# Second attention of a two-layer decoder: the gate chain over four engines, and the weighed sums formed in quarters

## The reference, cut to what matters

```
q, k, v = x@q_w + q_b, x@k_w + k_b, x@v_w + v_b      # 16 heads of 8
gate    = 1/(1+exp(-(g0 + ...)))                      # per query and head, from q and grep_w
score   = q.k*scale + gate*rel_bias                   # 128 x 128 per head, and one column for bias_k
p       = softmax(score);  attn = p @ v               # 128 queries x 8 per head
out     = layernorm(x + attn@out_w + out_b)           # no gain or offset
```

## Time and profile before

| | |
|---|---|
| median of 3 runs | 5442.01 us (5440.87 to 5447.32) |
| the profiled execution | 5440.75 us, span 5438.9 us |
| second attention in the span | from about 2452 to about 3430 us |
| PE / DVE / ACT / POOL busy over the whole span | 77% / 66% / 41% / 35% |
| the pow of the gate chain (L1380), POOL | 2929 ns, once per sequence |
| Exp of a head's scores (L1572), ACT | 393 ns, 16 per sequence |

### The profile page before, as it was taken

How to read it: one execution, slowest core, us unless ns; L and a number is a source line. 1 busy time by engine, 2 the same in 40 slices (tenths; PEclk the granted TensorE clock), 3 DMA queues, 4 the chain that set the end, 5 groups by cost and what they waited for, 6 DMA issues and landing times. The chain is left out here.

```text
span 5438.9 us, 100417 instructions
## 1 busy us (share of the span) xinstructions
PE 4180.3 (77%) x31987; PEld 2761.0 (51%) x31987; DVE 3586.4 (66%) x9085; ACT 2216.1 (41%) x4986; POOL 1928.3 (35%) x2355
## 2 busy tenths in 40 slices
PE   7888888878885666637888889677773299999998
PEld 3555555555554444435666666566663144444443
DVE  6556565645554555537888887455556688888888
ACT  1444444431111222205666666222221255555555
POOL 1000000024540000007777777000000077777777
PEclk9999999985555555556766776666665599999999
DMA  2000000000100000010000000011111366666564
GB/s 61 9 8 8 10 8 8 8 18 28 29 21 26 23 23 23 23 40 17 13 14 14 13 14 9 28 31 31 29 30 37 93 152 136 134 132 133 134 138 99
DMA packets 261738, 245.27 MB, mean 45 GB/s; under 512 B 28491, under 2 KB 188016, under 8 KB 261490
## 3 DMA queue, kind: packets, MB, share of 16 engines
q1 hardware_dynamic: 252402, 239.73, 18.3%
q10 hardware_dynamic: 9216, 4.20, 0.3%
HBM read 210.27 MB, written 33.55 MB: 45 GB/s over the span
## 5 line engine op out<-in xcount | busy, mean ns | idle before, releaser
L2324 POOL TENSOR_TENSOR d_hidden<-d_gated,d_upper 128x512 f32<-128x512 f32 x528 | 803.7, 1547 | 244.8 <-DVE d_upper L2433 103.1
L2440 DVE TENSOR_TENSOR d_h_low<-d_hidden,d_h_high 128x512 f16<-128x512 f32 x528 | 540.2, 1023 | 135.2 <-ACT d_h_high L2400 133.6
L2394 ACT ACTIVATE d_gated<-d_g 128x512 f32<-128x512 f32 x528 | 315.2, 597 | 479.8 <-PE d_u L2340 455.3
L2433 DVE TENSOR_TENSOR d_upper<-d_u,d_coef 128x512 f32<-128x512 f32 x512 | 349.0, 682 | 31.4 <-DMA d_coef<-coefT 11.8
L706 POOL MEMSET f_minus_half<- 128x1 f32 x1 | 0.1, 98 | 1027.5 <-POOLq L37 1027.5
L1572 ACT ACTIVATE c_sc<-c_sc,c_negmax 128x129 f32<-128x129 f32 x1024 | 326.3, 393 | 15.1 <-issue 11.9
L2400 ACT ACTIVATE d_h_high<-d_hidden 128x512 f16<-128x512 f32 x528 | 328.4, 622 | 8.2 <-POOL d_hidden L2324 8.2
L129 POOL TENSOR_TENSOR b_rstd<-b_var_eps,b_minus_half 128x1 f32<-128x1 f32 x128 | 67.1, 549 | 664.4 <-DVE b_var_eps L119 664.4
L129 POOL TENSOR_TENSOR d_rstd<-d_var_eps,d_minus_half 128x1 f32<-128x1 f32 x64 | 34.1, 548 | 677.4 <-DVE d_var_eps L119 677.4
L1392 POOL TENSOR_TENSOR c_posg<-w_pos,c_gate 128x512 f32<-128x512 f32 x256 | 265.7, 1039 | 3.1 <-issue 3.1
L2338 PE MATMUL d_g<-d_x_high,w_Wg_high 128*128 128x512 f16 x528 | 201.1, 381 | 83.7 <-POOL d_x_low L2317 38.7
(11 more groups left out here) (408 smaller groups left out, 11610.4 us busy)
## 6 DMA issues: line engine op xcount, KB each, us to landing
d_coef<-coefT SPq DMA_DIRECT2D x256, 512.0 KB, 7.6
mx_x<-in_xT SPq DMA_DIRECT2D x16, 256.0 KB, 2.8
b_x<-in_x SPq DMA_DIRECT2D x64, 64.0 KB, 1.8
y<-b_y SPq DMA_DIRECT2D x64, 64.0 KB, 1.6
f_y<-y SPq DMA_DIRECT2D x64, 64.0 KB, 1.9
f_x<-in_x SPq DMA_DIRECT2D x64, 64.0 KB, 1.9
x<-f_res SPq DMA_DIRECT2D x64, 64.0 KB, 1.5
b_x<-x SPq DMA_DIRECT2D x64, 64.0 KB, 1.8
```

The source lines that it names most:

```text
L2324: nc.gpsimd.tensor_tensor(hidden[b][:], gated[b][:], upper[b][:], ALU.mult).then_inc(h_ready, 1)
L2394: nc.scalar.activation(gated[b][:], ps_g[i][:], ACT.Silu, scale=1.0 / W_SCALE).then_inc(silu_ready, 1)
L2433: nc.vector.tensor_tensor(upper[b][:], ps_u[i][:], coef[c % CBUFS][:, u % CU, :], ALU.mult).then_inc(upper_ready, 1)
L2440: nc.vector.tensor_tensor(h_low[b][:], hidden[b][:], h_high[b][:], ALU.subtract).then_inc(h_low_ready, 1)
```

## The change

It has three parts, all in `phase_attn1`.

1. The gate chain. The Exp stays on ACT; the addition of 1 moves from POOL to ACT (an Identity with bias 1.0); the reciprocal moves from a pow with -1 on POOL to a reciprocal on DVE (`invert_gates`, in quarter 1 after `bias`). The small multiplication that fills `gate_rhs` moves from DVE, after its big transpose, to POOL (`gate_columns`, first in quarter 0 of the next column), and PE's `gates_and_values` waits for it.
2. `weigh` is split in four. Quarter `a` of the heads is weighed in quarter `a` of the column, the last part at the place where all 16 stood.
3. `combine`, `turn_attn` and `output` write the free half of the bank `ahead` (columns 256 to 511) instead of `back`. For that PE gets waits on `kv_next_ready`, `x_added` and `attn_ready`, and parts change places. PE: `project` goes from the front of quarter 1 to its end, `turn_attn` from quarter 1 to 2, `output` from 2 to 3. ACT: `copy_attn` from quarter 1 to the end of quarter 2, `norm` from 0 to 1, `store` from 1 to 2. DVE: `add_x` from quarter 2 to after `turn_rows` in 3. POOL: `power` from the end of 3 to quarter 0 of the next column.

The unused branches around `SHIFTED` (an empty tuple before) go too. The diff, cut to its core:

```diff
 # POOL
+    def gate_columns(it, j):
+        pool.wait_ge(rows_ready, nth(it, j))
+        nc.gpsimd.tensor_tensor(gate_rhs[s][:, :, 4:8], rows[s][:, NEXT, 0:4]..., w["quarter"]..., ALU.mult).then_inc(rhs_ready, 1)
     def gates(it, j):
-        nc.gpsimd.tensor_scalar(gate[s][:], gate[s][:], 1.0, None, ALU.add).then_inc(gate_added, 1)
-        nc.gpsimd.tensor_tensor(gate[s][:], gate[s][:], minus_ones[:], ALU.pow).then_inc(gate_inverted, 1)
         pool.wait_ge(gate_inverted, nth(it, j))
 # PE
     def project(it, j):
+        if not is_early(it, j, 4):
+            pe.wait_ge(attn_ready, nth(it, j) - 4)
     def gates_and_values(it, j):
-        pe.wait_ge(rows_ready, nth(it, j))
+        pe.wait_ge(rhs_ready, nth(it, j))
-    def weigh(it, j):
+    def weigh(it, j, a):
+        if a == 0:
+            pe.wait_ge(v_ready, nth(it, j))
+            if not is_early(it, j, 1):
+                pe.wait_ge(weighed_copied, nth(it, j) - 1)
+        pe.wait_ge(pT_copied, quarter(it, j, a))
+        for i in range(4):
+            last = nc.tensor.matmul(back[32 * i:32 * i + 32, a * T:(a + 1) * T], ...)
     def combine(it, j):
+        pe.wait_ge(x_added, nth(it, j) - 1)
+        pe.wait_ge(kv_next_ready, nth(it, j) + 3)
-        out = back[:, 128:128 + H * (HD + 1)]
+        out = ahead[:, 256:256 + H * (HD + 1)]
     def turn_attn(it, j):
+        pe.wait_ge(kv_next_ready, nth(it, j) + 4)
-        nc.tensor.transpose(back[:, 0:T], ...)
+        nc.tensor.transpose(ahead[:, 256:384], ...)
     def step(...):
         if a == 0:
             run(gates_and_values, ahead1)
+            run(weigh, behind1, 0)
             run(combine, behind2)
         if a == 1:
-            run(project, ahead2)
             run(scores, column, 2)
             run(turn, behind1, 3)
-            run(turn_attn, behind2)
+            run(weigh, behind1, 1)
+            run(project, ahead2)
         if a == 2:
             run(scores, column, 3)
             run(turn, column, 0)
-            run(output, behind2)
+            run(weigh, behind1, 2)
+            run(turn_attn, behind2)
         if a == 3:
             run(scores, ahead1, 0)
             run(turn, column, 1)
+            run(output, behind2)
             run(turn_last, behind1)
-            run(weigh, behind1)
+            run(weigh, behind1, 3)
 # ACT
+    act.wait_ge(gate_exp, nth(it, j))
+    nc.scalar.activation(gate[s][:], gate[s][:], ACT.Identity, bias=1.0).then_inc(gate_added, 1)
 # DVE
+    def invert_gates(it, j):
+        dve.wait_ge(gate_added, nth(it, j))
+        nc.vector.reciprocal(gate[s][:], gate[s][:]).then_inc(gate_inverted, 1)
```

More of the change, by code:

```diff
@@ L1323, in pv @@
         def pv(out):
-            return back[:, 128:128 + H * (HD + 1)].rearrange("p (h e) -> p h e", h=H)[out]
+            return ahead[:, 256:256 + H * (HD + 1)].rearrange("p (h e) -> p h e", h=H)[out]
         EVERY = slice(0, P)
@@ L1412, in step @@
                 def step(a, ahead2, ahead1, column, behind1, behind2, behind3):
+                    if a == 0:
+                        run(gate_columns, ahead1)
                     if a == 2:
@@ L1512, in turn_attn @@
                     pe.wait_ge(attn_ready, nth(it, j))
-                    nc.tensor.transpose(back[:, 0:T], attn[slot(j)][:].rearrange("p h e -> p (h e)"), w["ident"][:]).then_inc(attnT_ready, 1)
+                    if not (isinstance(it, int) and U * it + j >= S - 4):
+                        pe.wait_ge(kv_next_ready, nth(it, j) + 4)
+                    nc.tensor.transpose(ahead[:, 256:384], attn[slot(j)][:].rearrange("p h e -> p (h e)"), w["ident"][:]).then_inc(attnT_ready, 1)
                 def output(it, j):
                     pe.wait_ge(attnT_copied, nth(it, j))
-                    nc.tensor.matmul(back[:, 128:128 + D], attnT[slot(j)][:], w["out_w"][:], start=True, stop=True).then_inc(out_ready, 1)
+                    nc.tensor.matmul(ahead[:, 384:512], attnT[slot(j)][:], w["out_w"][:], start=True, stop=True).then_inc(out_ready, 1)
                 def step(a, ahead2, ahead1, column, behind1, behind2, behind3):
@@ L1592, in copy_attn @@
                     act.wait_ge(attnT_ready, nth(it, j))
-                    nc.scalar.activation(attnT[slot(j)][:], back[:, 0:T], ACT.Copy).then_inc(attnT_copied, 1)
+                    nc.scalar.activation(attnT[slot(j)][:], ahead[:, 256:384], ACT.Copy).then_inc(attnT_copied, 1)
                 def norm(it, j):
@@ L1617, in step @@
                         run(copy_turned, behind1, 3)
-                        run(copy_attn, behind2)
-                        run(store, behind3)
+                        run(norm, behind3)
                     if a == 2:
@@ L1623, in step @@
                         run(copy_turned, column, 0)
+                        run(store, behind3)
+                        run(copy_attn, behind2)
                     if a == 3:
@@ L1659, in turn_rows @@
                 def turn_rows(it, j):
[L1660 removed]
+                    s = slot(j)
                     dve.wait_ge(low_ready, nth(it, j))
[L1662 to L1665 removed]
+                    nc.vector.transpose(rows[s][:].rearrange("p b t -> p (b t)"), padded[s][:].rearrange("p b t -> p (b t)")).then_inc(rows_ready, 1)
+                def invert_gates(it, j):
+                    s = slot(j)
+                    dve.wait_ge(gate_added, nth(it, j))
+                    nc.vector.reciprocal(gate[s][:], gate[s][:]).then_inc(gate_inverted, 1)
                 def last_score(it, j):
@@ L1714, in step @@
                         run(bias, column, 1)
+                        run(invert_gates, ahead1)
                         run(project, ahead2)
@@ L1719, in step @@
                         run(choose, ahead2)
-                        run(add_x, behind2)
                     if a == 3:
@@ L1723, in step @@
                         run(turn_rows, ahead2)
+                        run(add_x, behind2)
                 pipelined(nc.vector, step)
```

80 lines of the change are left out of this document (28 added, 52 removed).

## The result

| | before | changed |
|---|---|---|
| median | 5441.44 us (5438.9 to 5447.32, 4 runs) | 5577.45 us (5575.62 to 5580.83, 4 runs) |
| changed to before | | 1.0249, 95% interval 1.0231 to 1.0267 |

The account below looks back on a forecast made before the run. Bound: a cycle through PE and DVE. The column goes from 14.44 to 16.2 us (16.6 less clock gain); 62 x 1.76 = 109 us on 5440.75 gives 5550, median 5551; 8-in-10 range 5475 to 5600.

Parts of the forecast that it names:

- The cycle through PE's project, DVE's project and choose: Second attention before: PE's and DVE's `project`, `choose`, rows, gates, `combine` form one cycle, about 14 of 14.8 us.
- The two branches behind choose: After `choose`: rows ready at about 15.8 us; attention's output through `copy_attn` gives next gates at 16.6, setting the column.
- What the clock gives back: PE time at 2.4 GHz shortens the column from 16.6 towards 12.7 us; a tenth of 3.9 taken, giving 16.2.
- The signs named ahead: Expected changed profile: engine waits, POOL's share down about a fifth, columns 16 to 16.6 us, clock 0.65 or less.
- Rival (1): Second attention: quarters of `weigh` fill PE's gaps, PE mostly at 2.4 GHz, 12.7 us a column, 5334 us; chance 0.10.
- The gate chain: Second attention: `gate_rhs` to POOL gains some 0.4 us a column; pow leaving POOL nothing; DVE reciprocal 0.25 us, covered.
- Busy time and the clock: PE in the second attention: being busy does not lift the clock; busy 11.87 of 12 us, it stood at 0.50.

Follow-up runs that it names:

- weigh whole: Changed kernel with the four quarters of `weigh` together at the place of the last one, all else as changed: 5383.47 us, 0.9909 of before.
- the gate chain alone: Kernel before with only addition of 1 on ACT, reciprocal on DVE, `gate_rhs` on POOL: 5379.44 us, 0.9894 of before.
- `gate_rhs` alone: Kernel before with only `gate_rhs` moved from DVE to POOL, addition and pow staying on POOL: 5414.15 us, 0.9942 of before.

## Why the prediction was right, and where it was not

- **The cycle through PE's project, DVE's project and choose.** Right. At 1.2 GHz the reckoning had `project` end at 7.86, `choose` at 11.53, `copy_attn` at 13.24, the next gates at 16.6; measured 8.32, 12.00, 13.62, 16.87. The 0.46 up to `project` is 0.04 in each of two quarters of `weigh` (0.59 start to start, 0.55 taken), 0.15 in `combine` (2.33 against 2.18), 0.13 in the turn ahead of a quarter of `weigh` (1.04 against 0.91) and 0.08 in the gates. That a part behind another one begins later where a quarter of `weigh` follows it is a price of splitting that the reckoning lacked.
- **The two branches behind choose.** Right, and shown by moving `copy_attn`: the output's branch was 0.6 us later, 0.8 had been reckoned.
- **What the clock gives back.** This is the term that was mis-sized: a tenth of 3.9 us, 0.4, was taken. Most columns do have 3.4 us at 2.4 GHz, but behind `project`, and are as long as columns with none, 16.87; the mean gives back 0.05. With it and the 0.27 above, 16.2 became 16.82; that is the difference between the 109 us forecast for the stage and the 144 measured from the first gates to the last. That the whole program came nearer to the forecast, 136 us against 110, is luck: the last stage of the program was 15 us shorter, a term that the prediction did not have.
- **The signs named ahead.** The gates' wait gone (87.4 to 4.3 us), `output` waiting for ACT by over 1 us (88.4 us in 59), and a clock under 0.65 (0.58) came as said. DVE's wait for `project` was named too small, 1.5 us where it was 2.3 (141.4 in 61), and so was the one for `combine`, 1.5 where it was 2.1 (124.7 in 59). POOL's busy share in the window fell from 0.77 to 0.49, not by a fifth; and the columns, 16.82 us, are just above the 16 to 16.6.
- **Rival (1), TensorE mostly at 2.4 GHz.** Its number was right for the wrong kernel: it said that `weigh` in quarters fills PE's gaps and so lifts the clock. The experiments show the opposite: `weigh` in one piece lifts it to 0.82, in quarters it stands at 0.58 with PE as busy as before. The prediction treated order and clock as two terms to be added. They multiply: the late `project`, `copy_attn` and `output` cost 2.1 us a column at the lower clock (16.5 in the one full column of "weigh whole" at 0.60 against 14.4 for the gate chain alone), and next to nothing once `weigh` is whole and the clock up (13.70 against 13.61). So of the three parts of the change, the split of `weigh` decides over the sign.
- **The gate chain.** `gate_rhs` had been given 0.4 us a column, which the traces bear out: from the end of the transpose to the next gates it was 0.85 us in the mean before, and 0.38 with `gate_rhs` on POOL. The pow was given nothing, since work beside it hid it. No run takes the pow alone out of the kernel before, so what it cost there stays open; with `gate_rhs` moved it costs 0.26 us a column, through DVE's `negmax`, which hiding it beside other work had left out.
- **Busy time and the clock.** PE stood at 0.50 in a stretch in which it was busy 8.00 of 8.00 us, and at 1.00 in one in which it was busy 7.42 of 10.1. The Trainium skill ("TensorE: Matmul & The Clock Gate", the section on the clock gate) says that activity releases the throttle. If activity is read as busy time, the trace does not agree.

- **A version that beats both.** Five kernels are 1.1 to 1.2% faster than before, within 0.1% of each other, which these runs cannot tell apart; the gate chain alone (5379 us) is the plainest.

## What to carry to other kernels

Before you spread a block of matmuls over a loop to fill gaps, read at which parts of the loop the granted clock is high, and whether those lie on the cycle that sets the period; here one contiguous block of 16 heads was worth 194 us of a whole program over the same block in four pieces. A higher share at 2.4 GHz in the mean says little: 0.87 and 0.71 gave the same time here. In a software pipeline, look twice before moving a part that feeds a chain over several engines (project, choose, high parts, low parts, transpose) behind other work, or a copy that PE needs behind an instruction that waits for the same chain: undoing either gave 66 and 40 us here with `weigh` in quarters, and 8 us or nothing with `weigh` whole. An operation that seems hidden can still cost by what it pushes beside another engine's work, as the pow did. And test the parts of a change one by one: without the split of `weigh` this one is 0.9% faster than before, with it 2.5% slower.

## What was not expected of the hardware

TensorE's clock fell into patterns that repeat over columns, and a change of 0.5 us in one wait could be lost to another pattern: six kernels with clocks of 0.69 to 0.87 in the stage came out between 13.61 and 13.70 us a column. A scaling of 128 x 4 on DVE (`negmax`) takes 0.17 us alone and up to 1.06 beside POOL; in the timeline of `gate_rhs` alone above it starts at 2694.88 beside `gated_pos` (L1398, 2694.86 + 1.04) and ends with it. In that kernel its mean was the highest:

```profile
L1693 DVE TENSOR_SCALAR c_negmax<-c_top 128x4 f32<-128x4 f32 x173 | 82.2, 475 | 5.9
```

475 ns, against 371 with the gate chain alone. The Trainium skill ("SBUF — State Buffer", the section on the two separate sides) says that DVE, in an operation that uses its second pair of ports, and GpSimd exclude each other for the whole length of the instruction. Beside `gated_pos` the trace agrees. Beside the pow it does not: in the same kernel 43 `negmax` of 2600 to 3200 us start with 0.5 to 1.6 us of the pow (L1386) still to run, and every one takes 0.17 us, as the one at 2691.95 above does. Why the pow leaves DVE alone was not tried.
